# Slot 3 of an RK4 step, reordered bank by bank, with small row operations between

## What is computed

```python
def _derivative(q, p, drive, coupling, bias):
    i_couple = jnp.tanh(q) @ coupling.T
    dq = q - q ** 3 / 3.0 - p + drive + i_couple + bias
    dp = EPSILON * (q + ALPHA - BETA * p)
    return (dq, dp)

def _rk4_step(q, p, drive, coupling, bias):
    dq1, dp1 = _derivative(q, p, ...)
    dq2, dp2 = _derivative(q + 0.5 * DT * dq1, p + 0.5 * DT * dp1, ...)
    dq3, dp3 = _derivative(q + 0.5 * DT * dq2, p + 0.5 * DT * dp2, ...)
    dq4, dp4 = _derivative(q + DT * dq3, p + DT * dp3, ...)
    q_next = q + DT / 6.0 * (dq1 + 2 * dq2 + 2 * dq3 + dq4)
    ...
```

## Time and profile before

| | |
|---|---|
| median of 3 runs | 617.65 us (617.12 to 618.13) |
| profiled execution | 617.41 us |
| its span, first to last instruction | 615.4 us |
| seeds of slot 0 (L1026), first and last | 308.9 and 592.8 us |
| busy: PE, DVE, ACT, POOL | 580.3, 516.1, 401.7, 255.7 us |
| granted PE clock, mean | 0.997 |

### The profile page before, as it was taken

How to read it: one execution, slowest core, us unless ns; L and a number is a source line. 1 busy time by engine, 2 the same in 40 slices (tenths; PEclk the granted TensorE clock), 3 DMA queues, 4 the chain that set the end, 5 groups by cost and what they waited for, 6 DMA issues and landing times.

```text
span 615.4 us, 14209 instructions
## 1 busy us (share of the span) xinstructions
PE 580.3 (94%) x4918; PEld 525.5 (85%) x4918; DVE 516.1 (84%) x1544; ACT 401.7 (65%) x968; POOL 255.7 (42%) x401
## 2 busy tenths in 40 slices
PE   8899999999999879998888999999999999999997
PEld 7899999999999878887776888888888887888885
DVE  2776767776767768888988999999999999999996
ACT  2545454544445456575447888897888888788785
POOL 0333323232332353420144555555565565565550
PEclk9999999999999999998999999999999999999999
DMA  8400000000000000500000000000000000000001
GB/s 272 164 2 2 1 1 2 1 1 2 1 1 1 19 1 1 186 1 1 2 0 2 10 11 18 19 10 18 19 15 15 19 19 10 18 20 11 17 19 35
DMA packets 12517, 14.87 MB, mean 24 GB/s; under 512 B 1632, under 2 KB 10144, under 8 KB 12448
## 3 DMA queue, kind: packets, MB, share of 16 engines
q1 hardware_dynamic: 12448, 13.97, 6.7%
HBM read 9.78 MB, written 4.19 MB: 23 GB/s over the span
## 4 chain that ended last, share of the span: by engine, by line
PE 63%; DVE 16%; ACT 14%; issue 4%; SPq 1%; DMA 1%; POOL 0%; ACTq 0%; DVEq 0%
PE PS L451 18%; PE PS L313 16%; PE PS L336 12%; ACT q_s L756 4%; PE PS L503 3%; PE PS L524 3%; ACT k_s L737 2%; PE PS L429 2%; PE PS L389 2%; PE PS L487 2%; PE PS L372 2%; ACT big L669 2%; ACT q_s L798 2%; DVE h_s L1056 1%; DVE big L938 1%
## 5 line engine op out<-in xcount | busy, mean ns | idle before, releaser
L451 PE MATMUL PS<-k_s,h_s 128*128 128x128 f32 x1024 | 160.7, 285 | 4.5 <-DVE PS L1036 1.9
L451 PEld LDWEIGHTS PS<-k_s,h_s 128*128 128x128 f32 x1024 | 131.7, 191 | 21.7 <-DVE PS L1044 9.7
L313 PE MATMUL PS<-part 128*128 128x256 f32 x900 | 115.6, 286 | 0.7 <-issue 0.7
L313 PEld LDWEIGHTS PS<-part 128*128 128x128 f32 x900 | 109.8, 191 | 0.9 <-issue 0.9
L737 ACT ACTIVATE k_s<-h_s 128x128 f32<-128x128 f32 x256 | 68.8, 305 | 41.1 <-DVE h_s L1056 33.7
L336 PE MATMUL PS<-big,wrk 128*128 128x128 f32 x744 | 88.4, 275 | 3.0 <-DVE big L895 3.0
L336 PEld LDWEIGHTS PS<-big,wrk 128*128 128x128 f32 x744 | 85.8, 192 | 3.6 <-DVE big L895 3.6
L1204 POOL COPY h_s<-big 128x256 f32<-128x256 f32 x32 | 21.4, 670 | 131.0 <-DVE big L895 131.0
L451 PE MATMUL PS<-h_s 128*128 128x128 f32 x384 | 74.2, 275 | 0.0
L451 PEld LDWEIGHTS PS<-h_s 128*128 128x128 f32 x384 | 58.3, 192 | 0.0
L634 ACT ACTIVATE big<-big 128x256 f32<-128x256 f32 x32 | 13.3, 416 | 65.6 <-DVE big L877 65.6
(11 more groups left out here) (184 smaller groups left out, 1270.9 us busy)
## 6 DMA issues: line engine op xcount, KB each, us to landing
out<-q_s SPq DMA_DIRECT2D x32, 128.0 KB, 1.7
x_s<-in_xT SPq DMA_DIRECT2D x14, 256.0 KB, 6.1
k_s<-in_wgT SPq DMA_DIRECT2D x1, 832.0 KB, 5.8
k_s<-in_wuT SPq DMA_DIRECT2D x1, 832.0 KB, 7.4
k_s<-in_wih SPq DMA_DIRECT2D x3, 256.0 KB, 4.4
wrk<-in_whh SPq DMA_DIRECT2D x3, 256.0 KB, 4.8
h_s<-in_wdT SPq DMA_DIRECT2D x1, 768.0 KB, 6.4
x_s<-in_xT SPq DMA_DIRECT2D x4, 128.0 KB, 3.6
```

The source lines that it names most:

```text
L313: r = pe.matmul(p, y, x, start=i == 0, stop=i == len(passes) - 1)
L451: return pe.matmul(PS[:, m, 0:128], w, x, start=False, stop=True, skip_group_check=True)
```

## The change

Four things, all in slot 3 of each time step.
- `nexts` of slot 2 and `seed_4` are taken apart: bank 0's eviction, bank 0's seed, bank 1's eviction, bank 1's seed. `seed_4` now has its three waits at both banks.
- The single operation on the row maximum that made two scales is split in two with one source tensor each: a 1-column `tensor_scalar` for the first scale ahead of the eviction of slot 2, and one by wmean ahead of the evictions of slot 3, with a semaphore s_h2 of its own, for which ACT's output scaling now waits. The reciprocal goes between bank 0's eviction and seed.
- t4 goes ahead of the slot's cubic term, directly behind t3.
- PE takes slot 3's products in another order: identity and first product of bank 0, then of bank 1 when its seed is there, then the second product of bank 0 and of bank 1.

```diff
--- before.py
+++ after.py
@@ -212,7 +212,7 @@
         s_q0, s_cb, s_mag, s_cp = sem("s_q0"), sem("s_cb"), sem("s_mag"), sem("s_cp")
         s_x1t, s_x1k, s_dr = sem("s_x1t"), sem("s_x1k"), sem("s_dr")
         s_th, s_sq, s_w, s_ps, s_next, s_seed = (sem(n) for n in ("s_th", "s_sq", "s_w", "s_ps", "s_next", "s_seed"))
-        s_t3, s_t4, s_p, s_q = (sem(n) for n in ("s_t3", "s_t4", "s_p", "s_q"))
+        s_t3, s_t4, s_p, s_q, s_h2 = (sem(n) for n in ("s_t3", "s_t4", "s_p", "s_q", "s_h2"))
         s_u3, s_uz, s_v1, s_W3, s_WZ, s_dq, s_t1, s_t2 = (
             sem(n) for n in ("s_u3", "s_uz", "s_v1", "s_W3", "s_WZ", "s_dq", "s_t1", "s_t2"))
         s_turnq, s_turnqi, s_gate, s_up, s_turnh, s_down = (
@@ -526,7 +526,17 @@
                     r.then_inc(s_gate, 1)
 
 
-                coupled(4 * t + 3, id_z3, qs[1])
+                slot, w = 4 * t + 3, th[1]
+                pe.wait_ge(s_seed, 2 * slot + 1)
+                add(0, id_z3, cm(qs[1], 0))
+                pe.wait_ge(s_th, 2 * slot + 1)
+                add(0, coupU[:, 0, 0:128], cm(w, 0))
+                pe.wait_ge(s_seed, 2 * slot + 2)
+                add(1, id_z3, cm(qs[1], 1))
+                add(1, coupU[:, 0, 128:256], cm(w, 0))
+                pe.wait_ge(s_th, 2 * slot + 2)
+                add(0, coupU[:, 1, 0:128], cm(w, 1)).then_inc(s_ps, 1)
+                add(1, coupU[:, 1, 128:256], cm(w, 1)).then_inc(s_ps, 1)
                 if t == 0:
                     keep_warm(7, 3)
                 if t >= 2:
@@ -795,6 +805,7 @@
                         ac.wait_ge(s_st[i % 2], 16 * (i // 2))
                     ac.wait_ge(s_down, i + 1)
                     ac.wait_ge(s_x1t, min(i + 2, T))
+                    ac.wait_ge(s_h2, i + 1)
                     ac.activation(ob[i % 2], po, ACT.Copy, scale=h_at(i, 2)).then_inc(s_osc, 1)
 
             def middle(i, a=0, b=NI):
@@ -1036,22 +1047,21 @@
                 ve.scalar_tensor_tensor(PS[:, m, 0:128], cm(qn[t % 2], m), (1 + 2 * A * kap) / (2 * c4), cm(W3, m),
                                         ALU.mult, ALU.add).then_inc(s_seed, 1)
 
-            def seed_4(t):
+            def seed_4(t, m):
                 ve.wait_ge(s_dq, t + 1)
                 ve.wait_ge(s_WZ, t + 1)
-                for m in range(2):
-                    ve.wait_ge(s_next, 8 * t + 5 + m)
-                    ve.scalar_tensor_tensor(PS[:, m, 0:128], cm(dq, m), 1 / c4, cm(WZ, m), ALU.mult,
-                                            ALU.add).then_inc(s_seed, 1)
+                ve.wait_ge(s_next, 8 * t + 5 + m)
+                ve.scalar_tensor_tensor(PS[:, m, 0:128], cm(dq, m), 1 / c4, cm(WZ, m), ALU.mult,
+                                        ALU.add).then_inc(s_seed, 1)
 
             def cubic(slot, src):
                 s = slot % 4
                 ve.wait_ge(s_sq, slot + 1)
                 ve.scalar_tensor_tensor(w_, sqP, cube[s] * own[s], src, ALU.subtract, ALU.mult).then_inc(s_w, 1)
 
-            def nexts(slot, dst):
+            def nexts(slot, dst, ms=(0, 1)):
                 ve.wait_ge(s_w, slot + 1)
-                for m in range(2):
+                for m in ms:
                     ve.wait_ge(s_ps, 2 * slot + m + 1)
                     ve.scalar_tensor_tensor(dst(m), PS[:, m, 0:128], of_ps[slot % 4], cm(w_, m), ALU.mult,
                                             ALU.subtract).then_inc(s_next, 1)
@@ -1115,26 +1125,29 @@
                     ve.wait_ge(s_hN, 2 * i + 2)
                     ve.tensor_reduce(h_at(i, 0), hN[i % 2], X, ALU.max, apply_absolute_value=True).then_inc(s_mxh, 1)
                 cubic(4 * t + 2, qs[1])
-                nexts(4 * t + 2, lambda m: cm(qs[2], m))
-
-
-                seed_4(t)
                 if t >= 2:
                     ve.wait_ge(s_mxh, i + 1)
-                    ve.scalar_tensor_tensor(h_at(i, 1, 2), wide(h_at(i, 0), 2), TINY, wvec[:, 3:5], ALU.max,
-                                            ALU.mult).then_inc(s_thh, 1)
+                    ve.tensor_scalar(h_at(i, 1), h_at(i, 0), TINY, 1.0 / 127.0, ALU.max, ALU.mult).then_inc(s_thh, 1)
+
+
+                nexts(4 * t + 2, lambda m: cm(qs[2], m), (0,))
+                if t >= 2:
+                    ve.wait_ge(s_thh, i + 1)
+                    ve.reciprocal(h_at(i, 4), h_at(i, 1)).then_inc(s_s2, 1)
+                seed_4(t, 0)
+                nexts(4 * t + 2, lambda m: cm(qs[2], m), (1,))
+                seed_4(t, 1)
                 if t < T - 1:
                     ve.wait_ge(s_t2, t + 1)
                     ve.wait_ge(s_next, 8 * t + 4)
                     ve.scalar_tensor_tensor(t3, t2, horner[2], qs[1], ALU.mult, ALU.add).then_inc(s_t3, 1)
-                cubic(4 * t + 3, qs[2])
-                if t < T - 1:
                     ve.wait_ge(s_t3, t + 1)
                     ve.wait_ge(s_next, 8 * t + 6)
                     ve.scalar_tensor_tensor(t4, t3, horner[3], qs[2], ALU.mult, ALU.add).then_inc(s_t4, 1)
+                cubic(4 * t + 3, qs[2])
                 if t >= 2:
                     ve.wait_ge(s_thh, i + 1)
-                    ve.reciprocal(h_at(i, 4), h_at(i, 1)).then_inc(s_s2, 1)
+                    ve.tensor_scalar(h_at(i, 2), h_at(i, 1), wmean[:, 2:3], None, ALU.mult).then_inc(s_h2, 1)
                 nexts(4 * t + 3, lambda m: PS[:, m, 128:256])
                 for m in range(2):
                     ve.wait_ge(s_next, 8 * t + 7 + m)
```

## The result

| | before | after |
|---|---|---|
| median of 4 runs each | 617.89 us (617.12 to 618.76) | 624.46 us (623.25 to 624.65) |
| ratio | 1 | 1.0105 (95% interval 1.0087 to 1.0122) |
| profiled execution, its span | 617.41, 615.4 us | 624.37, 622.5 us |

A forecast was written before the change was run, and what follows sets the result against it. It took a tight PE and DVE relay in each step as the bound, with DVE becoming late in slot 3: 31 x 0.20 + 0.11 = 6.3 us on 617.41, plus 0.24 for the median, gave 624.0 us; range 620.5 to 626.2.

The forecast's parts named there:

- The circle: Each step's PE and DVE hand-overs are tight; DVE has 0.24 us spare, only in slot 3.
- The price of a fresh result: Slot 3 seeds behind their evictions: bounds 0.04 us (operation waits itself) and 0.13 (three semaphores, wait instruction); 0.13 taken.
- Items 1 and 2: New 1-column operation ahead of slot 2's first eviction, reciprocal behind it: both hidden in dependence waits, cost 0.
- Items 3 to 5: Slot 3's first seed at 526.41, slot 2's second eviction at 526.61, slot 3's second seed at 527.03 us.
- Item 6: t3 at 527.23, t4 directly behind it waits for its result and starts at 527.69: cost 0.12 us.
- Item 7: Cubic term at 528.02, then the second new operation ahead of slot 3's first eviction: cost 0 to 0.01 us.
- Item 8: Slot 3's evictions at 528.47 and 528.67, DVE late instead of PE: 0.20 us more in each step.
- The last step: The last step has no t3 and t4, so PE decides: 0.11 us later than before.
- The sum: Whole kernel: 31 x 0.20 + 0.11 = 6.3 us slower, median 624.0 us.
- That the wait instruction costs nothing: Rival: slot 3 seeds start 0.04 behind a fresh result; 0.6 us more in all, 618.3 us; chance 10%.
- That dependent operations follow at the plain spacing: Rival: no extra wait behind fresh results on DVE, PE decides; 7 us faster, 610.6 us; chance 4%.
- ScalarE: Rival: ScalarE falls behind, L798 waits for it in drive-block steps; about 1 us more, 625.2 us; chance 10%.

The follow-up runs named there:

- e8: Kernel before with only t4 moved directly behind t3: step 9.08, 617.89 us, ratio 0.9996.
- e1: Changed kernel with s_next held by the slot 3 seed itself instead of its wait instruction: step 9.11, 618.58 us, ratio 1.0015 to the kernel before.
- e10: Changed kernel with its first new 1-column operation written with a second source tensor: step 9.44, 627.64 us, ratio 1.0153 to the kernel before.
- e9: e7 with the two scales made again by two single-source operations: step 9.06, 616.70 us, ratio 0.9985 to the kernel before.
- e2: Changed kernel with t4 put back behind the cubic term: step 9.25, 622.71 us, ratio 1.0076 to the kernel before.
- e5: Changed kernel with both scales made by one two-source operation of 2 columns: step 9.43, 629.24 us, ratio 1.0176 to the kernel before.
- e6: Changed kernel with the edits of e1, e2 and e5 together: step 9.20, 621.29 us, ratio 1.0047 to the kernel before.
- e12: e9 with the second scale operation (by wmean) moved between bank 1's eviction and seed: step 9.06, 616.42 us, ratio 0.9978 to the kernel before.
- e7: e6 with PE finishing bank 0 before bank 1's coupling products: step 9.20, 621.35 us, ratio 1.0047 to the kernel before.

## Why the prediction was right

Point by point, by its own steps:

- **The circle** (PE and DVE alternate, DVE has 0.24 to spare in slot 3 and nowhere else): right. e8 shows the slack by using half of it for nothing. In the changed kernel VectorE no longer stands idle for PE in slots 2 and 3. A small wait is left that no bracket shows: the second eviction of slot 1 starts 0.23 behind the first (528.99 to 529.22) where 0.20 would do; it is 0.22 to 0.24 in both kernels.
- **The price of a fresh result:** 0.04 held by the operation, 0.13 through the wait instruction of 50 ns: right, and the one term that decides. e1 isolates it: 0.20 a step for two seeds, where 2 x 0.09 = 0.18 was the difference. The ground for it was thinner than the prediction has it. In the step at 516.97 the second eviction lies between, at 517.18, and 0.21 behind that one is 517.39 as well: the row can't tell 0.13 from less. The pair of the first stage carries the weight. The trace of the kernel before has better rows, the wait instructions themselves: in 30 of 32 steps L1043 starts 38 or 39 ns behind the end of bank 0's eviction and lasts 50. In the changed kernel the seed starts 45 ns behind its wait instruction's end, together 0.13.
- **Items 1 and 2** (small operations hidden in a dependence gap): right, 0.45 from cubic term to eviction with and without. I had not asked what makes them fit. Had the first had two SBUF sources, it would have cost 0.13 a step (e10). The prediction's row for a small operation, 526.88, was taken while GpSimd was idle (it is in all 30 steps); it was luck that the form of the new one made this irrelevant.
- **Items 3 to 5:** forecast 0.87, 1.07 and 1.49 behind the cubic term, measured 0.88, 1.08 and 1.51.
- **Item 6**, t4: forecast 2.15, measured 2.17.
- **Item 7:** the second operation's bounds were 0.07 and 0.13; it costs 0.13 (524.29 to 524.42), the upper one, of which all but 0.01 lies in the wait for the cubic term: the eviction is 0.46 behind the cubic term, and 0.45 without such an operation. The forecast was 0 to 0.01.
- **Item 8:** the evictions were forecast 2.93 and 3.13 behind the cubic term, and are 2.97 and 3.17 behind. The step is 9.30 instead of 9.27. The 0.03 to 0.04 is the term that I had too small: an operation behind one that waited stands 0.21 and not 0.20 behind it (the earlier trace rows had that, from 528.47 to 528.68), and the cubic term 0.34 and not 0.33 behind t4. Over 31 steps that is 1 us more.
- **The last step:** forecast 0.11 later by PE, counted from the first eviction of slot 2; measured 0.18 (bank 1's last eviction 2.48 behind it before, 2.66 after). Bank 0's eviction waits for PE's fifth product, and bank 1's stands 0.21 behind it.
- **The sum** gave 6.3 us; the spans differ by 7.1 and the medians by 6.6. Between the profiled executions it is 6.96. The steps alone give 31 x 0.23 = 7.1 where 6.2 were forecast, so the size was 0.03 a step too small; that the medians came as near as 6.6 to 6.3 is in part the scatter of four runs each.
- **The rivals.** That the wait instruction costs nothing: refuted by e1. That dependent operations follow at the plain spacing: refuted by the 0.45 and 0.46 in every step of both kernels. The Trainium skill's "VectorE: DVE Perf Modes" (The DRAIN you can't avoid) reports that a semaphore behind each of 8 copies costs nothing extra. The traces here don't agree for operations this small: the dependence costs 0.12, and where the semaphore is waited for decides 0.10 more. ScalarE: it decided nothing in the changed kernel (no mark of it in the step), but it did in e9, by 0.08 at the cubic term.

What stays open: the 0.23 us that a step got longer is not divided fully. Undoing the wait's place gives back 0.20 and undoing t4's place 0.06, together more than the whole. The gains don't add up, since PE stands right behind VectorE and is late next (e2 shows it for t4's place). No run undoes the bank by bank order alone, or moves only the reciprocal.

## What to carry to other kernels

Putting an operation directly behind the one whose result it reads costs a wait that the plain spacing of operations doesn't have (0.12 us here), and the price rises (to 0.22) if that result is waited for in a wait instruction of its own: let the operation itself hold the semaphore that is raised last, and leave the long-raised ones to the wait instruction (in this kernel the order of three source lines, 0.20 of 9.31 us a step). Before using a dependence gap for small work, look at what GpSimd does at that time, and if it runs, give the operation one SBUF source at most. And before an engine's order is tightened, ask whether it is the late one there: the same stall of 0.12 cost nothing where PE was late (e8) and 0.06 where it no longer was (e2).

## What was not expected of the hardware

A VectorE operation with two SBUF source tensors that starts while GpSimd runs an operation is held up by it. One of 1 or 2 columns took 0.34 instead of 0.15 us behind GpSimd's 0.73 us subtraction and ended 14 to 20 ns behind it (60 of 60 in e5 and e6). A seed, 128 columns, that met GpSimd's constant multiplication of p took 0.34 instead of 0.29 and ended 0.14 to 0.15 behind GpSimd's end (30 of 30 in e12). So what is left to do behind GpSimd's end grows with the columns. That it is the reading of the sources that waits is my inference from these two; it fits that a seed still took 0.29 where GpSimd ended 0.15 behind the seed's start (e9), and 0.34 where it was 0.19 and 0.20 (e12, e7). An operation with one SBUF source was untouched at the same place (0.14 in all 30 steps of the changed kernel), and so were the evictions, with one source in SBUF and one in PSUM.

The kernel before has it too, where I hadn't looked: of its 64 seeds of slot 1, one took 0.43 (at 310.68) and one 0.39 (at 320.68) instead of 0.29, both with GpSimd running. The other way round GpSimd is held up: its addition in slot 1, which starts while a seed has 0.20 to run, takes 0.78 in 30 of 32 steps of the kernel before, and 0.73 in the two where no seed runs or one has only 0.13 left.

The Trainium skill ("SBUF — State Buffer", Who interferes with whom) states this: a VectorE instruction with two SBUF inputs contends with a GpSimd instruction that reads SBUF, since its second input comes through the read interface that the two share; one with at most one SBUF input, outside the 2-port modes, doesn't contend; and the order of issue decides who blocks. The traces agree with all three, by the numbers above. I should have drawn on it in the prediction, as a check on items 1 and 7.
